# One addition for both heads of a pair, two accumulators side by side in place of three; eight key tiles in the first pair and six in the fifth added up on VectorE

## The reference

```python
# layer 0: x = x + attention(group_norm(x)); 12 heads of 64 channels, N = 1024 positions
qkv = x_flat @ W_qkv.T
q, k, v = (qkv[0], qkv[1], qkv[2])
var_v = jnp.var(v, axis=-1, ddof=1, keepdims=True)
var_k = jnp.var(k, axis=-1, ddof=1, keepdims=True)
scores = var_v @ jnp.swapaxes(var_k, -2, -1) * scale
attn = jax.nn.softmax(scores, axis=-1)
out = attn @ v
...
out = out @ W_proj.T + b_proj
# layer 1: x = x + displace(group_norm(x)): shift each channel group by a window, then a 3x3 kernel
```

## Time and profile before

| what | value |
|---|---|
| median of three runs | 2066.14 us |
| the profiled execution's own time | 2068.55 us |
| its span, first to last instruction | 2066.8 us |
| mean granted TensorE clock | 0.994 |
| PE busy | 2002.8 us, 97% |
| DVE busy | 1668.6 us, 81% |
| ACT busy | 1207.0 us, 58% |
| POOL busy | 264.3 us, 13% |
| one batch after another, in steady state | 244 to 248 us |

### The profile page before, as it was taken

The page is one execution under the profiler, slowest core; times in us unless marked ns, Lnnn a source line. Parts: engine busy times, 40 slices in busy tenths (PEclk is TensorE's granted clock), DMA queues, the critical chain, the costliest instruction groups (busy, mean ns, idle before and its releaser), DMA issues.

```text
span 2066.8 us, 33759 instructions
## 1 busy us (share of the span) xinstructions
PE 2002.8 (97%) x12924; PEld 1115.2 (54%) x12924; DVE 1668.6 (81%) x3594; ACT 1207.0 (58%) x1321; POOL 264.3 (13%) x323
## 2 busy tenths in 40 slices
PE   3999999999999999999999999999999999999997
PEld 3756347662565536554376634766256553655443
DVE  6688576997679976898769987699867997699857
ACT  3576734776267743778527783477626774377820
POOL 2100001111012100111001210111101210011121
PEclk9999999999999999999999999999999999999998
DMA  8212303445044541446114561344603454144514
GB/s 324 83 53 63 103 1 102 133 130 180 2 124 144 162 116 42 126 129 205 45 63 126 158 178 22 99 130 133 184 2 124 144 162 116 42 128 132 147 35 183
DMA packets 104978, 236.33 MB, mean 114 GB/s; under 512 B 46704, under 2 KB 47472, under 8 KB 104816
## 3 DMA queue, kind: packets, MB, share of 16 engines
q0 software_dynamic: 31968, 116.41, 19.4%
q1 hardware_dynamic: 66800, 95.74, 15.3%
q10 hardware_dynamic: 6048, 22.02, 3.1%
HBM read 154.06 MB, written 79.73 MB: 113 GB/s over the span
## 4 chain that ended last, share of the span: by engine, by line
PE 58%; DVE 20%; DMA 8%; issue 7%; ACT 5%; SPq 1%; ACTq 0%; POOL 0%; DVEq 0%; POOLq 0%
PE ps L1303 23%; PE ps L1360 16%; PE ps L1345 14%; DVE bt L885 7%; ACT ring L671 5%; DVE st L837 3%; DMA a_sb<-a_rows 3%; PE ps L1320 2%; DMA dt_sb<-d_sb 2%; DMA a_rows<-at 1%; DVE bst_x L811 1%; DMA bt<-r_rows 1%; DVE bt L1008 1%; DVE bt L1005 1%; SPq L447 1%
## 5 line engine op out<-in xcount | busy, mean ns | idle before, releaser
L671 ACT ACTIVATE ring<-a_sb,coef 128x1024 f32<-128x1024 f32 x768 | 817.7, 1137 | 23.5 <-issue 12.3
L1303 PE MATMUL ps<-wkv_hi,h_sp 128*128 128x256 f16 x4608 | 771.8, 273 | 3.9 <-DVE h_sp L828 2.4
L1345 PE MATMUL ps<-ring,xv 128*64 128x512 f32 x3072 | 691.3, 597 | 6.2 <-ACT ring L671 5.1
L1303 PE MATMUL ps<-wkv_lo,h_sp 128*128 128x256 f16 x2304 | 628.8, 273 | 0.0
L885 DVE TENSOR_TENSOR bt<-bt,ring 128x1024 f32<-128x1024 f32 x464 | 541.8, 1212 | 3.0 <-ACT ring L671 1.7
L1303 PEld LDWEIGHTS ps<-wkv_hi,h_sp 128*128 128x128 f16 x4608 | 451.5, 98 | 85.5 <-issue 28.5
L1345 PEld LDWEIGHTS ps<-ring,xv 128*64 128x64 f32 x3072 | 207.7, 137 | 427.0 <-issue 385.1
L655 ACT ACTIVATE xv<-ps 128x256 f32<-128x256 f32 x192 | 72.7, 383 | 511.8 <-DVE st L837 510.9
L1360 PE MATMUL ps<-xv,wp_hi 128*128 128x512 f16 x1152 | 349.7, 380 | 0.0
L837 DVE BATCH_NORM_STATS2 st<-ps 128x6 f32<-128x64 f32 x1536 | 217.0, 211 | 123.4 <-PE ps L1303 122.6
L1303 PEld LDWEIGHTS ps<-wkv_lo,h_sp 128*128 128x128 f16 x2304 | 225.7, 98 | 26.6
(11 more groups left out here) (164 smaller groups left out, 1397.9 us busy)
## 6 DMA issues: line engine op xcount, KB each, us to landing
a_sb<-a_rows SPq DMA_DIRECT2D x96, 512.0 KB, 5.4
out<-xv POOLq DMA_DIRECT2D x84, 512.0 KB, 5.3
xv<-in_x POOLq DMA_DIRECT2D x48, 512.0 KB, 3.7
h_sp<-in_x ACTq DMA_DIRECT2D x42, 512.0 KB, 5.3
shift_rows<-bt POOLq DMA_DIRECT2D x42, 512.0 KB, 3.4
bt<-r_rows SPq DMA_DIRECT2D x80, 256.0 KB, 4.0
shift_rows<-ring SPq DMA_DIRECT2D x12, 528.0 KB, 15.3
xv<-in_L_conv_W_qkv SPq DMA_DIRECT2D x4, 1152.0 KB, 14.2
```

The lines of the kernel that those rows point to most:

```text
L671: nc.scalar.activation(ring_of(p, s, m), a_sb[:, h % 4, :], ACT.Exp, scale=coef[:, h, m:m + 1]).then_inc(s_exp, 1)
L1303: last = nc.tensor.matmul(ps[:, kv_bank[u % 2], half * 2 * P:(half + 1) * 2 * P], h_sp[:, k, hp, m * P:(m + 1) * P], wkv[wpart][:, k, q * ...
L1345: last = nc.tensor.matmul(ps[s * HD:(s + 1) * HD, o_bank[p % 2] + j, :], v_sb[:, p, m, s * HD:(s + 1) * HD], ring_of(p, s, m)[:, j * HALF: ...
```

## The change: one wide addition per key tile

Two things change together. The two additions of a key tile (one for each head, 128x1024) become one of 128x2048: the slots of both heads lie next to each other in the ring, and the two accumulators next to each other in `bt`; the third accumulator is no longer used. And MD goes from (7, 8, 8, 8, 5, 5) to (8, 8, 8, 8, 6, 5): key tile 7 of pair 0 and key tile 5 of pair 4 go from PE to DVE.

```diff
+        acc2 = bt[:, 0:2 * N]
...
-        MD = (7, 8, 8, 8, 5, 5)
+        MD = (8, 8, 8, 8, 6, 5)
...
-            ADDS_TO.append(ADDS_TO[-1] + 2 * (n - 1))
+            ADDS_TO.append(ADDS_TO[-1] + n - 1)
...
-            return ADDS_TO[p] + 2 * (max(m, 1) - 1) + s + 1
+            return ADDS_TO[p] + max(m, 1)
...
-            return acc[:, (2 * p + s) % NA_RING, :]
+            return acc[:, s, :]
+
+        def both_of(p, m):
+            i = (p * MT + m) * 2 % RING
+            return ring_flat[:, i * N:(i + 2) * N]
...
-                for s in (0, 1):
-                    i = (p * MT + m) * 2 + s
-                    if m == 1:
-                        if s and (later or p):
-                            dve.wait_ge(s_d, b * NP + p)
-                        one = ring_of(p, s, 0)
-                    else:
-                        dve.wait_ge(s_acc, b * NADD + add_count(p, s, m - 1))
-                        one = acc_of(p, s)
-                    dve.wait_ge(s_exp, b * NT + i + 1)
-                    nc.vector.tensor_tensor(acc_of(p, s), one, ring_of(p, s, m), ALU.add).then_inc(s_acc, 1)
+                if m == 1:
+                    if later or p:
+                        dve.wait_ge(s_d, b * NP + p)
+                    one = both_of(p, 0)
+                else:
+                    dve.wait_ge(s_acc, b * NADD + add_count(p, m - 1))
+                    one = acc2
+                dve.wait_ge(s_exp, b * NT + (p * MT + m) * 2 + 2)
+                nc.vector.tensor_tensor(acc2, one, both_of(p, m), ALU.add).then_inc(s_acc, 1)
```

More of the change, by code:

```diff
@@ L319, in run, with add_count, acc_of @@
             last(B - 1)
-        MD = (7, 8, 8, 8, 5, 5)
+        MD = (8, 8, 8, 8, 6, 5)
         ADDS_TO = [0]
         for n in MD:
-            ADDS_TO.append(ADDS_TO[-1] + 2 * (n - 1))
+            ADDS_TO.append(ADDS_TO[-1] + n - 1)
         NADD = ADDS_TO[NP]
-        def add_count(p, s, m):
-            return ADDS_TO[p] + 2 * (max(m, 1) - 1) + s + 1
-        def acc_of(p, s):
-            return acc[:, (2 * p + s) % NA_RING, :]
+        def add_count(p, m):
+            return ADDS_TO[p] + max(m, 1)
+        def acc_of(s):
+            return acc[:, s, :]
+        def both_of(p, m):
+            i = (p * MT + m) * 2 % RING
+            return ring_flat[:, i * N:(i + 2) * N]
         def ring_of(p, s, m):
@@ L669, in exps @@
                         if mj < MD[pj]:
-                            act.wait_ge(s_acc, b * NADD + add_count(pj, s, mj))
+                            act.wait_ge(s_acc, b * NADD + add_count(pj, mj))
                     nc.scalar.activation(ring_of(p, s, m), a_sb[:, h % 4, :], ACT.Exp,
@@ L1394, in span @@
                         d_bank_free(b, p, later)
-                    denominators([acc_of(p, s) for s in (0, 1)], MD[p] == MT, True).then_inc(s_d, 1)
+                    denominators([acc_of(s) for s in (0, 1)], MD[p] == MT, True).then_inc(s_d, 1)
             def r_spread(b):
```

## The result

The changed kernel takes 2085.82 us (median of 4 runs, 2083.16 to 2089.82), the kernel before 2066.81 (4 runs, 2064.36 to 2068.34). The ratio on record is 1.0077, with a 95% interval of 1.0056 to 1.0098; the two medians alone are 19.0 us or 0.92% apart, which lies inside that interval. The forecast was 2079 in a range of 2070 to 2088: the direction and the place were right, the size of 13 us was too small by 6. The profiled execution took 2089.82 us with a span of 2088.1. In the series behind this one, one run of `wide_only` (2620.17 us) and one of the kernel before beside it (5347.8 us) fell in a slower state of the chip and are left out of the medians.

A forecast was written before the change was run, and what follows sets the result against it. PE and DVE were taken to end pair 0 together, with pair 5 waiting on the query rows' transfers. Later batches 8.5 us, less 1.7 and 0.5, plus 6.9 for the clock, made +13.2 on 2066.14: 2079 us, range 2070 to 2088.

The forecast's parts named there:

- The addition: On DVE: a 2048-column addition lasts 2.28 us and advances DVE by 2.20, or 2.32 when the next needs its result.
- rival of cheap additions: Each wide addition saves 0.14 us, so pair 0's stall is 0.68 us shorter per batch: 2074.5 us, chance 8%.
- The stall in pair 0: End of pair 0: PE idles 2.28 us for DVE's seventh addition; next kv unit 1.46 us later, +10.2 us in seven batches.
- The credits: End of pair 1: PE, itself 1.46 us later, no longer waits for DVE, which gives back 1.7 us.
- Pairs 1 to 3: PE's lateness passes through these pairs; DVE's first addition of pair 4 is held by PE, 1.22 us later than before.
- Pair 4 and 5: Pair 4 loses 1.14 us on PE, counted at nothing in seven later batches because pair 5 waits for the query rows.
- The sign that would have spoken against the forecast: Start of pair 5's exponentials not moving with PE would show the forecast wrong.
- The clock behind the stall: After pair 0's stall the clock falls in four of seven batches, 1.72 us each: +6.9 us, bounds none to 12.0.
- the sum over the projection: A later batch is 1.22 to 1.46 us longer; no term was added for the projection.
- falls in every batch: Rival: the clock falls behind pair 0's stall in every later batch, +18.3 us, 2084.5 us; chance 8%.
- dear additions: Rival: a wide addition costs twice the narrow one, 2.43 us, adding 7.4 us in pair 0: 2086.7 us; chance 6%.

The follow-up runs named there:

- wide_only: The changed kernel's wide additions with the old shares (7, 8, 8, 8, 5, 5): 2065.91 us, ratio 0.9996 to the kernel before.
- wide_p0: Wide additions with only pair 0's tile moved to DVE, (8, 8, 8, 8, 5, 5): 2077.65 us, ratio 1.0054 to the kernel before.
- wide_p4: Wide additions with only pair 4's tile moved to DVE, (7, 8, 8, 8, 6, 5): 2071.61 us, ratio 1.0022 to the kernel before.
- both_fixes: Changed kernel with pair 0's accumulator ones-matmuls behind pair 1's first kv unit and `r_spread` two short projection pieces later: 2071.26 us, ratio 1.0016 to the kernel before.
- both_p0: Same two moves as both_fixes, but with shares (8, 8, 8, 8, 5, 5), so pair 4's tile stays on PE: 2067.34 us, ratio 0.9998 to the kernel before.
- spread_p4: wide_p4 with `r_spread` two short pieces of the projection later on PE: 2068.85 us, ratio 1.0001 to the kernel before.
- spread_only: wide_only with `r_spread` two short pieces of the projection later on PE: 2068.13 us, ratio 1.0006 to the kernel before.
- xload_p4: spread_p4 with the loads of the next batch's x issued in pair 4 moved to pair 5: 2072.33 us, ratio 1.0028 to the kernel before.
- filler_p0: Changed kernel with 18 redundant matmuls on PE in front of the wait at the end of pair 0: 2077.55 us, ratio 1.0039 to the kernel before.
- narrow_md: Kernel before, with its narrow additions and three accumulators, given the new shares (8, 8, 8, 8, 6, 5): 2087.62 us, ratio 1.0098 to the kernel before.
- defer_p0: Changed kernel with pair 0's accumulator ones-matmuls moved behind pair 1's first kv unit on PE: 2077.12 us, ratio 1.0039 to the kernel before.

## Why the prediction was right, and where it was short

**The addition.** Right. 2.281 us by the groups against the 2.28 worked out, and two that depend on one another start 2.32 us apart (585.42 and 587.74). The rival of cheap additions is out: by its rule, "The DRAIN you can't avoid" in VectorE: DVE Perf Modes of the Trainium skill, the narrow ones cost their full duration and the wide form would bring 0.94 us in pair 0. The trace disagrees: the wait with narrow additions is 2.50 us and with wide ones 2.28, 0.22 apart, where I had worked out 0.18 for six tiles and 0.25 with the seventh. The section itself goes on that a next operation that isn't held starts earlier; the prediction took its rule without that sentence, and successive narrow additions 1.135 us apart at a length of 1.212 fit that sentence.

**The stall in pair 0.** Right: 2.27 to 2.29 us of idle time in all seven later batches, forecast 2.28. The next kv unit starts 609.39 - 605.34 = 4.05 us after the last key tile. 2.28 of it are the wait and 1.76 the ones-matmuls, which take 0.97 at full clock; so 0.8 us of the clock's price is already in it. Without that it is 3.25, against 607.63 - 605.84 = 1.79 before: the 1.46 us worked out. In the first batch the wait was 0.28 us, and PE won about 0.6 us where 0.5 was assumed.

**The credits.** Right in kind, too large in size: at the end of pair 1 PE waited once, 1.18 us, where before it waited 1.7 in all. With what led up to that wait, 0.3 us came back and not 1.7.

**Pairs 1 to 3.** The wait of DVE's first addition in pair 4 is there, ended by PE (timeline of DVE, against the earlier trace rows):

```profile
703.59 2.29 DVE L888 TENSOR_TENSOR bt<-ring 128x2048 f32<-128x2048 f32 x1 [0.92 <-PE ps L1323]
```

It is not what decided: pairs 2 and 3 take PE the same 434.9 us.

**Pair 4 and 5.** Right in effect. 1.15 us a batch went from pair 4 and nothing came of it, in four pairs of kernels that differ in this alone: changed kernel against wide_p0 and wide_p4 against wide_only, each slower by 0.2 to 0.3%, both_fixes against both_p0 (0.18%, from two series) and spread_p4 against spread_only (level, from two series). The percentages are by the ratios on record; by the medians the first pair is 0.4% apart. The sign that would have spoken against the forecast didn't come: in the third batch the query rows' write leaves 13.17 us behind the end of pair 3 on PE, before and after (713.00 - 699.83 and 715.62 - 702.45), so it moves with PE. And taking the tile out of pair 4 didn't bring the exponentials of pair 5 nearer: they start 24.1 us behind the end of pair 3 in wide_p4 and 24.2 in wide_only, on average over the seven later batches, while PE is through with pair 4 1.15 us earlier. In the changed kernel pair 5 is no longer than in the kernel before (174.3 against 175.4), but 5.1 us longer than in wide_p0, and the stretch behind it 6.9. The reason was told only in part: xload_p4 shows that behind the query rows' way comes that of the denominators and reciprocals, and that the loads of x slow whichever of the two they run beside. The tile itself the prediction priced at 1.14 us with a key tile of 1.72; its own row, 7.02 us for four, gives 1.76 and so 1.10. Measured are 26.38 - 25.23 = 1.15 us.

**The clock behind the stall.** Four falls of 1.72 us were assumed; five came, and each cost 32.71 - 31.06 = 1.65 us in pair 1. filler_p0 shows this term by itself. That it was five is not fixed by the length of the stall: other executions with the same stall had two (wide_p0) and five (narrow_md).

**The step that was mis-sized** is the sum over the projection. I carried a later batch's length from pair 0 to pair 5 and counted the projection as unchanged, with nothing for the wait at `r_spread` although show it with a fall of the clock behind it. The profiled execution has 6.5 us more there and falls of the clock behind five of these waits, where the one before has one. The stretch from `r_spread` to the end of pair 0 is 20.5 us longer, of which 7 x 1.46 = 10.2 are the stall. Batch by batch it shows the rest: before, 92.9 us in six batches and 94.6 in the one with a fall; after, 94.4 and 94.9 in the two without a fall, 96.1 in three with one, and 97.6 and 97.7 in the two where it lasted twice as long. Together that is the other 10.3. How much of this belongs to the medians is less sure, since single executions differ: wide_only's has 8.2 us of such waits and is level with before. The mean granted clock of the timed runs doesn't settle it: it is 0.990 for the changed kernel and 0.993 for the kernel before in the first series, 0.991 for filler_p0 and 0.990 for defer_p0, and some executions (wide_p0, wide_p4, filler_p0, defer_p0) also have a long stretch at 1.2 GHz at 32 us, ahead of the attention, that hardly moves the end of pair 0 in the first batch. So the waits and falls at `r_spread` are shown for one execution, and their share in the medians stays open.

What the medians leave of the account is this: 19.0 us, of which pair 0 is 12 by wide_p0 (stall and clock together) and pair 4's table entry 5 to 6 by wide_p4; the 1 to 2 left over are less than the uncertainty of each, some 3 us, as the intervals say. Pair 4's part is just what the prediction had counted at nothing; it also had 6.9 us for the clock where 8.2 came. The terms that were off, pair 4, the clock and the credits, all lay on one side, and that the time is still inside the range is luck in part: it lies 2 us from an upper edge that had been set for other reasons, falls in every batch and dear additions.

## What to carry to other kernels

When two engines end a stage together, as here, work moved from the fuller one to the other makes a stall of the whole added instruction, and the saving must be set against that, not against the engine's share of the span. Ask of each stall on TensorE what runs behind it: a wait of two us here cost another 1.65 us in matmuls at half clock, and dummy matmuls in the wait brought just this back. Where a saved step is followed by a wait for a chain of transfers, count the step at nothing until a run shows otherwise; and after moving an instruction to fill one wait, look for the wait that it makes further on.

## What the runs showed that I had not expected

- Equal waits of 2.27 to 2.29 us had a fall to 1.2 GHz behind them in five cases and none in two, in one execution; the matmuls behind all seven are the same ones. A wait of 1.54 us had a fall (0.57 at 761 us), one of 1.18 us at the end of pair 1 none (mean clock 1.00 from 1640 to 1644). In wide_p0's execution the same seven waits (2.26 to 2.27 us) had a fall behind two, in narrow_md's (2.49 to 2.51 us) behind five. What decides I can't say.
- The eight matmuls over one row that spread the reciprocals (L1406) took 1.09 us at full clock before, and 1.37 and 1.98 us where the clock was falling or down.
- Taking 0.88 us of matmuls from PE in each batch, with PE at 96%, changed nothing in both_p0. PE's high share says here that it works in most stretches, not that it sets their pace.
